# Attribute transfers that wait for a scatter pair's landing from group 5 and 6 on instead of from group 9 and 10

## The reference, cut to what matters

```
node_features[col]                                   # gather, one row of x per edge (col = dst)
s1 = einsum('ea,eb,abc->ec', xs, es, W1)             # scalar x scalar
s2 = einsum('eai,ebi,abc->ec', xv, ev, W2)           # vector . vector
v1 = einsum('ea,ebi,abc->eci', xs, ev, W3)           # scalar x vector
v2 = einsum('eai,eb,abc->eci', xv, es, W4)           # vector x scalar
messages = concat(out_s, out_v) @ Wm + bm
agg = segment_sum(messages, row, num_segments=50000) # scatter-add (row = src)
upd = concat([node_features, agg], -1) @ Wu + bu
return layernorm(x + (x + upd))
```

## Time and profile before

| | |
|---|---|
| median of three runs | 1809.12 us (1806.32 to 1816.49) |
| profiled execution | 1798.85 us, span 1797.0 us |
| DVE busy | 1570.2 us, 87% |
| PE busy | 1576.2 us, 88% |
| POOL busy | 1097.9 us, 61% |
| DMA engines, mean rate | 266 GB/s over the span |
| first `times_xs` of slot 5, 10 and 97 | 146.28, 241.79 and 1498.13 us |

### The profile page before, as it was taken

One profiled execution on the slowest core, in us unless ns is written; L12 is line 12 of the kernel. 1 busy time (PEld: TensorE's weight loads), 2 busy tenths in 40 slices (PEclk: granted clock), 3 DMA queues, 4 the chain that ended last, 5 costly groups with the idle time before them and its releaser, 6 DMA issues.

```text
span 1797.0 us, 35490 instructions
## 1 busy us (share of the span) xinstructions
PE 1576.2 (88%) x11572; PEld 874.3 (49%) x11572; DVE 1570.2 (87%) x1726; ACT 977.3 (54%) x2015; POOL 1097.9 (61%) x837
## 2 busy tenths in 40 slices
PE   4177889999999999999999999999999999388882
PEld 2033444544555555455555545545455554376662
DVE  6275789999999999999999999999999996299994
ACT  1123545555655555555555555555555555188884
POOL 3005777777777777777778777777777774211110
PEclk8688999999999999999999999999999999699996
DMA  9996578888888888888888888888888886899994
GB/s 377 399 392 176 137 229 237 245 245 250 249 243 256 242 241 250 244 258 242 251 249 242 244 246 250 247 240 243 251 240 244 239 253 170 289 400 420 414 420 156
DMA packets 174618, 477.23 MB, mean 266 GB/s; under 512 B 48664, under 2 KB 111640, under 8 KB 149484
## 3 DMA queue, kind: packets, MB, share of 16 engines
q1 hardware_dynamic: 91980, 366.58, 56.0%
q0 software_dynamic: 82304, 109.12, 28.2%
q10 hardware_dynamic: 288, 0.95, 0.2%
HBM read 380.25 MB, written 96.31 MB: 265 GB/s over the span
## 4 chain that ended last, share of the span: by engine, by line
DMA 38%; issue 25%; POOL 21%; DVE 10%; PE 2%; ACT 1%; SPq 1%; POOLq 1%; DVEq 0%; ACTq 0%
DMA agg<-summed,row_idx 24%; POOL agg L356 13%; POOL xg L338 7%; DMA prod<-agg 6%; DMA e_sb<-in_e_rep 4%; DMA agg<-start_rows 4%; DVE prod L555 3%; DVE prod L613 2%; DVE stats L632 2%; DVE prod L543 2%; DVE mv L638 1%; DMA xg<-in_x_rows,dst_sb 1%; PE ps L688 0%; ACT prod L498 0%; PE ps L676 0%
## 5 line engine op out<-in xcount | busy, mean ns | idle before, releaser
L356 POOL DMA_INDIRECT agg<-summed,row_idx x392 | 625.9, 1597 | 290.8 <-issue 150.5
L555 DVE TENSOR_TENSOR prod<-ps,e_sb 128x2048 f32<-128x2048 f32 x294 | 655.0, 2282 | 77.9 <-DMA e_sb<-in_e_rep 55.0
L695 PE MATMUL ps<-prod,packed_sb 128*32 128x512 f32 x2744 | 671.6, 606 | 0.8 <-ACT S_sb L410 0.8
L338 POOL DMA_INDIRECT xg<-in_x_rows,dst_sb x392 | 445.6, 1137 | 187.5 <-issue 103.6
L688 PE MATMUL ps<-prod,packed_sb 128*32 128x512 f32 x2352 | 396.4, 603 | 0.0
L563 DVE TENSOR_TENSOR prod<-ps,e_sb 128x3072 f32<-128x3072 f32 x98 | 328.0, 3347 | 0.0
L543 DVE TENSOR_TENSOR prod<-ps,e_sb 128x2048 f32<-128x2048 f32 x98 | 223.5, 2281 | 50.2 <-issue 31.3
L453 ACT ACTIVATE summed<-ps 128x644 f32<-128x644 f32 x98 | 69.4, 708 | 306.9 <-PE ps L753 303.4
L676 PEld LDWEIGHTS ps<-packed_sb,spread 128*128 128x128 f32 x1176 | 127.2, 142 | 199.5 <-DVE prod L555 95.3
L676 PE MATMUL ps<-packed_sb,spread 128*128 128x128 f32 x1176 | 173.5, 285 | 31.0 <-DVE prod L555 23.9
L498 ACT ACTIVATE prod<-prod,shift_n,rstd 128x160 f32<-128x160 f32 (+1 forms) x392 | 166.6, 507 | 42.3 <-DVE shift_n L625 42.3
(11 more groups left out here) (62 smaller groups left out, 1786.4 us busy)
## 6 DMA issues: line engine op xcount, KB each, us to landing
e_sb<-in_e_rep SPq DMA_DIRECT2D x98, 1536.0 KB
e_sb<-in_e_rep SPq DMA_DIRECT2D x98, 1024.0 KB
agg<-start_rows SPq DMA_DIRECT2D x49, 640.0 KB, 14.4
prod<-agg SPq DMA_DIRECT2D x48, 640.0 KB, 10.8
out<-prod POOLq DMA_DIRECT2D x48, 640.0 KB, 7.7
e_sb<-in_x_t SPq DMA_DIRECT2D x25, 640.0 KB, 11.1
prod<-in_x_t SPq DMA_DIRECT2D x24, 640.0 KB, 12.1
row_sb<-in_src_row SPq DMA_DIRECT2D x98, 128.0 KB
```

The lines of the kernel that those rows point to most:

```text
L338: nc.gpsimd.indirect_dma_start(xg[g[1] % 2][:, q, :], None, x_rows, bass.IndirectOffsetOnAxis(dst_sb[g[1]][:, q:q + 1].bitcast(U32), 0)).t ...
L356: nc.gpsimd.indirect_dma_start(agg, bass.IndirectOffsetOnAxis(row_idx[g[1]][:, q:q + 1].bitcast(U32), 0), summed[g[1]][:, q // 2, q % 2 * ...
L555: nc.vector.tensor_tensor(prod[g[1] % 2][:, 4 + 4 * i:8 + 4 * i, :].rearrange("p (a b) e -> p a b e", b=2), ps[:, t_bank(g, 1 + i), :].uns ...
L695: return nc.tensor.matmul(ps[32 * quarter:32 * quarter + 32, S_BANK, :], w[:, 32 * half:32 * half + 32], prod[g[1] % 2][:, tile, :], start ...
```

## The change

The condition under which the two transfers have their wait on `scattered_a` is lowered by four groups. The thresholds themselves stay. `at_least(g, n)` is true inside the loop, and in a slot that is written out if the group's number is at least n. So `load_ev(5)` to `load_ev(8)` and `load_es(6)` to `load_es(9)`, issued in SP's slots 4 to 7, get a wait that they did not have: eight transfers. Nothing in the loop changes, and no instruction is moved on any engine.

```diff
@@ -221,7 +221,7 @@
 
                     sp.wait_ge(multiplied, number(g) * USES - 2 * USES + 4)
                     hold(sp, sp_passed)
-                if at_least(g, 10):
+                if at_least(g, 6):
 
                     sp.wait_ge(scattered_a, number(g) * 32 - 5 * 32 + 32)
                     hold(sp, sp_passed)
@@ -232,7 +232,7 @@
                 if at_least(g, 2):
                     sp.wait_ge(multiplied, number(g) * USES - 2 * USES + 6)
                     hold(sp, sp_passed)
-                if at_least(g, 9):
+                if at_least(g, 5):
 
                     sp.wait_ge(scattered_a, number(g) * 32 - 4 * 32 + 16)
                     hold(sp, sp_passed)
```

## The result

| | before | after |
|---|---|---|
| median of six runs | 1809.05 us (1806.24 to 1816.49) | 1798.0 us (1795.87 to 1804.87) |
| ratio | | 0.9932, 95% interval 0.991 to 0.9954 |
| profiled execution | 1798.85 us, span 1797.0 | 1804.87 us, span 1803.1 |
| start of slot 10 on DVE | 241.79 us | 230.93 us |

The change makes the kernel faster by 0.7%, 11 us between the medians; 13 were forecast. The two profiled executions taken by themselves say the opposite: the profiled one of before was faster than all its other runs, that of after slower than the others of its kernel. So the spans can't be subtracted here, and I compare stage by stage, where the two agree well up to the start of slot 5 (146.28 and 146.13 us). The ratio is an estimate from the runs and not the quotient of the two medians, which would be 0.9939.

What follows compares the result with a forecast made beforehand. In the edge phase, DVE and the loop over scatters and attribute transfers were taken to limit each other closely. Slot 10 would start 10.9 or 14.8 us sooner, taken as 13: 1809.12 - 13 = 1796 us, range 1785 to 1809.

Steps and rivals of the forecast that it cites:

- Step 1: SP's slots 4 to 7: the new waits bind, so `load_ev(5)`, issued at 127.01 before, goes out at about 149.
- Step 2: End of the table: with attributes held back, POOL's first scatter comes 2 us sooner (0 to 3.8), at 132.2.
- Step 3: POOL's first scatter pairs: with no attribute transfer under way, a pair follows the last after 6.6 us, before 8.4.
- Step 4: DVE in slot 5: `times_xv` waits for attributes until 157.6, 5.8 us later; slot 6 starts 3.7 us later.
- Step 5: Slots 6 to 9 take the loop's rhythm, 15.43 or 14.44 us each, from slot 6's start at 169.2.
- Step 6: DVE in slot 9: the 9.89 us stall is gone, since SP's waits are in phase with the scatters.
- rival D: Loop from slot 10 locks into a later phase, 14.83 instead of 14.44 us a slot: slower, 1832 us; chance 0.08.
- B: The stall only moves: slots 6 to 8 stay at 17.05 us, gain 4.4 us, time 1805; chance 0.14.
- C: Only lateness counts: slot 5's gap is added, slot 9's idle time stays, cost 3.7 us, time 1813; chance 0.08.

Runs made afterwards that it cites:

- the lower thresholds: Changed kernel with both `scattered_a` wait thresholds lowered by 16, one scatter pair, in the loop too; ratio 0.9946 to the kernel before (0.9925 to 0.9968).
- no wait at all: Both wait conditions set to `if False:`, so no attribute transfer waits for a scatter, in the loop neither; ratio 1.0933 to the kernel before (1.0869 to 1.0998).

## Why the prediction was right, point by point

The direction, the mechanism and the size came out: 1798.0 against 1796.

Step 1, the wait binds: right. `load_ev(5)` went out at 150.70, forecast at 149.0.

Step 2, the table ends sooner: wrong. The first scatter stayed at 134.29 (134.19 before); I had taken 2 us. Here are the stretches 126 to 130 and 130 to 134 us, by the columns of the earlier trace rows, first of before, then of after:

```profile
126.00:130.00 4.00, 0.00 (x0) 0.00 (x0) 4.00 (x3) 0.00 (x0) 0.00 (x0) 1.00 0.85 295
130.00:134.00 4.00, 0.00 (x0) 0.00 (x0) 2.77 (x2) 0.00 (x0) 0.00 (x0) 0.61 0.93 367
```

```profile
126.00:130.00 4.00, 1.14 (x8) 0.00 (x0) 4.00 (x3) 0.00 (x0) 0.00 (x0) 0.82 0.69 249
130.00:134.00 4.00, 0.00 (x0) 0.00 (x0) 2.83 (x2) 0.00 (x0) 0.00 (x0) 0.61 0.16 60
```

With the attributes held back, the 16 DMA engines are busy only 0.16 of the last 4 us, and the table still ends at the same time. A mean share of 0.16 is the work of two or three engines out of 16. The records of single packets in the trace show the tail: after the change 16 table packets are under way at 126.3, 4 at 130.8 and 2 at 132.3, and the sixteen landings of the last full piece are spread from 126.8 to 133.0. In the kernel before they are spread from 126.8 to 132.9, and at 131.2 there are again 4 table packets, beside 12 of the attributes. The table's tail hangs on a few engines that still have pieces queued, and in the kernel before the attributes only filled the others. My sum had taken the mean rate for a shared pipe: bytes / 402 GB/s. The row with 322 GB/s had the sign of it, since a pipe that everything waits for would not have slowed.

Step 3, pairs at POOL's own speed: right, 6.4 us against 6.6.

Step 4, slot 5 waits: right in kind. `times_xv` started at 158.54 against 157.6, the transfer took 7.8 us from its issue against 8.6; the price is 6.7 us instead of 5.8. The 2.1 us that step 2 had promised did not come, quicker pairs (0.4) and the quicker transfer (0.8) gave some of it back. The idle time was 7.87 us and not about 11, since slot 5 itself did not start sooner. Slot 6 started at 170.22, forecast 169.2.

Step 5, the loop's rhythm: right. Slots 6 to 9 took 15.18 us each, between the 14.44 and 15.43 that I had as ends. Slot 10 came at 230.93, at the upper end of 227.0 to 230.9.

Step 6, no stall of 9.89 us in slot 9: right, 2.10.

The sum of the stage is 10.9 us instead of 13. Step 2's term was too large by 2.1 us, and 2.0 us are missing, but that the two agree is luck. Slot 6 started only 1.0 us late, by the offsets of step 4; the other 1.0 is the rhythm of step 5, four slots of 15.18 us where the middle of my two values was 14.94. The last statement, that everything behind slot 10 only shifts, held in the medians but not in the profile: the 87 slots took 1273.5 us instead of 1256.3. I had named more than 1269 us as the mark of rival D. By it, and by the sentence that another time for the 87 slots would make the prediction wrong, the profile spoke against me. It was a bad mark, since the kernel before itself took 1269.6 in its second profile. From the start of slot 97 to the end nothing changed: 298.9 us before and 298.6 after.

As for the rivals, B is refuted: slots 6 to 8 went from 17.05 to 14.88 us ((214.87 - 170.22) / 3). C is refuted by the 2.10 us of slot 9 and by the median. On D, the locking into a slower pace, the medians leave room for at most a few us, as told above.

The Trainium skill's rule against the change (DMA: Bandwidth & Descriptors, Rules for kernel authors: issue early, wait late) is borne out by step 4's cost, a stall of 7.87 us in slot 5, and by nothing else here. The runs show what it leaves out: with every attribute transfer issued as early as it can be the kernel took 9.3% longer. The same page says in "Queues, rings and completion order" that a DMA engine takes turns between its queues packet by packet. This fits the pairs that take longer the more attribute bytes fall on them, but no run here shows the order of packets on one engine.

## What to carry to other kernels

A bulk transfer that is ready early is not free: if it falls on small scatters that a chain waits for, hold it until one of them has landed, and see that two bulk transfers don't fall on the same one. If such a pacing wait is in the loop, let it begin as soon as the loop's chain does; a few unpaced steps ahead of it build up a debt that is paid with a stall at the first wait. When an effect is some 10 us, compare the stage in which it acts, in two profiles of each kernel, before the spans. And compare it on the engine whose work ends the phase, here POOL's scatters: DVE's slot 10 promised 20 us for the lower thresholds and 11 for no wait at all, where the scatters had 12 and 0.

## What the runs showed of the hardware that was not expected

- A stream of equal writes ends unevenly over the DMA engines. In the last 4 us of the table the mean share of the 16 engines was 0.16 though no attribute transfer was in flight, and the sixteen landings of one piece were 6.2 us apart from first to last; holding back the 2560 KB issued behind it did not make it end sooner. Putting the 2560 KB issued ahead of its last pieces (`load_ev(4)` and `load_es(5)`) behind them did, by 7.4 us, where 2560 KB / 402 GB/s is 6.4 us.
- How two transfers are spread over the scatter pairs decides their landing: with one of 1024 or 1536 KB per pair the next pair followed after 6.7 to 8.6 us up to group 5, with both issued within 3 us of each other that pair or the next took 9.6 to 12.8. The share of time in which DMA was busy was lower in the slower kernel (0.78 against 0.85).
- The steady pace of one kernel differed by 0.15 us a slot between two executions (14.44 and 14.59), and the median of the kernel before by 12 us between chips (1798.9 and 1810.8), where a chip's own runs of it lie within 9 to 15 us.
